# TensorE's program as a loop over images instead of a straight list: a convolution attention and token attention kernel

## The reference, cut to what matters

```python
# layer 0, per image (x: 128 x 1024)
h = group_norm(x, norm_w, norm_b)
q, k, v = split(qkv_w @ h + qkv_b)
x = x + proj_w @ (softmax(q.T k * 128**-0.5) v) + proj_b
# layer 1, on tokens t = x.T (1024 x 128)
sq, sk, rv = heads(ln(t) @ wq_s), heads(ln(t) @ wk_s), heads(ln(t) @ wv_r)   # 8 heads of 16; rv: 2 of 16
retrieved = softmax(sq sk.T / 4) rv                                          # per head, both rv
t = t + mix(softmax over the two of (rq . (retrieved @ wk_ret)), retrieved) @ w_out
t = t + (ln(t) @ w_lora.T) @ ffn_W.T
```

## Time and profile before

| what | value |
|---|---|
| median of 3 runs (lowest, highest) | 4782.99 us (4782.89, 4784.51) |
| the profiled execution, and its span | 4781.04 us, 4779.3 us |
| busy, share of the span: PE, POOL, DVE, ACT | 96%, 89%, 81%, 68% |
| granted TensorE clock, mean | 0.984 of full |

### The profile page before, as it was taken

One profiled execution on the slowest core, in us unless ns is written; L12 is line 12 of the kernel. 1 busy time (PEld: TensorE's weight loads), 2 busy tenths in 40 slices (PEclk: granted clock), 3 DMA queues, 4 the chain that ended last, 5 costly groups with the idle time before them and its releaser, 6 DMA issues.

```text
span 4779.3 us, 95417 instructions
## 1 busy us (share of the span) xinstructions
PE 4587.4 (96%) x29230; PEld 2493.8 (52%) x29230; DVE 3881.3 (81%) x8190; ACT 3242.6 (68%) x6625; POOL 4238.1 (89%) x1142
## 2 busy tenths in 40 slices
PE   5999999999999999999999999999999999999986
PEld 4455555555555555555555555555555555555532
DVE  4788888888888888888888888888888888888773
ACT  2466777766777766777766777766777766777664
POOL 1599999999999999999999999999999999999996
PEclk8899999999999999999999999999999999999987
DMA  1111111111111111111111111111111111111110
GB/s 33 28 41 50 45 32 45 32 45 49 45 32 45 32 45 50 45 32 45 32 45 49 45 32 45 32 45 49 45 32 45 32 45 49 45 32 45 28 41 14
DMA packets 94729, 190.93 MB, mean 40 GB/s; under 512 B 17001, under 2 KB 53481, under 8 KB 94449
## 3 DMA queue, kind: packets, MB, share of 16 engines
q1 hardware_dynamic: 93008, 186.03, 14.0%
q10 hardware_dynamic: 1440, 0.55, 0.0%
HBM read 17.53 MB, written 16.78 MB: 7 GB/s over the span
## 4 chain that ended last, share of the span: by engine, by line
PE 91%; ACT 3%; DVE 2%; POOL 2%; issue 1%; DMA 0%; SPq 0%; ACTq 0%; DVEq 0%; POOLq 0%
PE ps_u L805 19%; PE ps_bank L771 14%; PE ps_bank L791 14%; PE ps_bank L754 10%; PE ps_bank L681 5%; PE ps_bank L692 4%; PE ps_bank L712 3%; PE ps_bank L740 3%; PE ps_bank L814 3%; PE ps_bank L743 3%; PE ps_bank L742 3%; PE ps_bank L741 3%; ACT p L965 2%; POOL p_sum L647 2%; PE ps_bank L723 2%; PE ps_bank L701 2%
## 5 line engine op out<-in xcount | busy, mean ns | idle before, releaser
L647 POOL TENSOR_TENSOR p_sum<-p_sum,p 128x2048 f32<-128x2048 f32 x768 | 3508.4, 4568 | 353.9 <-ACT p L965 306.0
L1085 DVE TENSOR_REDUCE max_part<-ps_bank 128x1 f32<-128x512 f32 x4096 | 2551.3, 681 | 573.5 <-PE ps_bank L771 563.3
L965 ACT ACTIVATE p<-ps_bank 128x512 f32<-128x512 f32 x4096 | 2160.9, 603 | 669.9 <-PE ps_bank L791 653.8
L805 PE MATMUL ps_u<-p,rv 128*32 128x512 f32 x8192 | 996.4, 604 | 0.9 <-ACT p L965 0.9
L771 PE MATMUL ps_bank<-k_stack,q_stack 63*128 63x512 f32 x4096 | 868.9, 452 | 55.2 <-ACT p L965 22.7
L791 PE MATMUL ps_bank<-q_stack,k_stack 64*128 64x512 f32 x4096 | 862.1, 453 | 49.5 <-ACT p L965 29.4
L771 PEld LDWEIGHTS ps_bank<-k_stack,q_stack 63*128 63x128 f32 x4096 | 387.6, 186 | 552.3 <-DVE max_part L1085 244.6
L791 PEld LDWEIGHTS ps_bank<-q_stack,k_stack 64*128 64x128 f32 x4096 | 372.9, 185 | 553.1 <-issue 321.7
L647 POOL TENSOR_TENSOR p_sum<-p 128x2048 f32<-128x2048 f32 x128 | 583.7, 4560 | 66.2 <-ACT p L965 66.2
L754 PE MATMUL ps_bank<-v,p 128*128 128x129 f32 x4096 | 506.8, 277 | 3.1 <-ACT p L920 1.6
L754 PEld LDWEIGHTS ps_bank<-v,p 128*128 128x128 f32 x4096 | 476.0, 191 | 50.1 <-issue 24.0
(11 more groups left out here) (143 smaller groups left out, 4231.8 us busy)
## 6 DMA issues: line engine op xcount, KB each, us to landing
k_stack<-k_hi SPq DMA_DIRECT2D x256, 128.0 KB, 2.6
q_stack<-q_hi SPq DMA_DIRECT2D x256, 128.0 KB, 2.8
x_sb<-in_x SPq DMA_DIRECT2D x32, 512.0 KB, 3.6
k_stack<-k_lo SPq DMA_DIRECT2D x128, 128.0 KB, 2.6
q_stack<-q_lo SPq DMA_DIRECT2D x128, 128.0 KB, 2.9
t_held<-t_front SPq DMA_DIRECT2D x32, 512.0 KB, 3.7
rqk<-tok_next SPq DMA_DIRECT2D x32, 512.0 KB, 3.6
t_core<-t_held SPq DMA_DIRECT2D x32, 512.0 KB, 2.9
```

Of the source, the lines that this page charges most:

```text
L647: pool.tensor_tensor(p_sum[:, phase % 2, :, :], before, p1[:, step % ring, :, :], ALU.add)\
L805: last = pe.matmul(ps_u[n * QUAD:(n + 1) * QUAD, :], rv[:, key_tile, :], p1[:, step % ring, n, :], start=(key_tile == 0), stop=(key_tile = ...
L965: act.activation(p1[:, step % ring, n, :], bank_of("scores", index // 2, n % 2), ACT.Exp, scale=scale1)\
L1085: dve.tensor_reduce(max_part1[:, phase % 2, i, n, half:half + 1], bank_of("max1", index // 2, side), AXIS.X, ALU.max)\
```

## The change

PE's program goes through the same branch of `in_order` as those of the other engines, and the parameter `loop` is gone.

```diff
-def in_order(nc, engine, order, images, stages, banks=None, links=None, section=SECTION, loop=True):
+def in_order(nc, engine, order, images, stages, banks=None, links=None, section=SECTION):
@@
     first = -min(ahead for _, _, ahead, _ in order)
     last = images - 1 - max(ahead for _, _, ahead, _ in order)
-    if not loop:
-        for b in range(last + 1 - images, first + images):
-            turn_of(b)
-        return
     for b in range(last + 1 - images, first):
         turn_of(b)
@@
                     "result": turn("result", t_core, result_ready, halves, out_ready),
-                }, banks, loop=False)
+                }, banks)
```

## The result

| | median (lowest, highest) |
|---|---|
| before | 4783.47 us (4782.16, 4786.09) |
| after | 4805.45 us (4803.32, 4813.21) |
| ratio | 1.0048, 95% interval 1.0038 to 1.0058 |

A forecast was written before the change was run, and what follows sets the result against it. PE was taken to bound the kernel, with 91% of the chain. Held handoffs 25, loop's end 0 and fetching 0 on 4781.0 us gave 4806, as a median 4808; 4807 was given, range 4779 to 4850.

The forecast's parts named there:

- held handoffs: Where PE is held by DVE or ACT: 44 holds a turn at 0.02 us each, 28 turns, 25 us more.
- loop's end: PE's branch behind den: taken as 0, covered by up to 2.8 us of queued array work; 18 us if uncovered.
- What bounds the kernel: Whole kernel: PE bounds it, with 91% of the chain and busy 141.23 of 143.37 us in a middle turn.
- Price of a register instruction: PE's sequencer: at most 0.11 us a step, from below nothing or a gain; 0.02 us taken per hold.
- step c: At held handoffs, the instruction carrying the wait also computes before the matmul: 0 to 0.11 us for each of 44 holds.
- Rival 2, faster: PE's handoffs: at 10 of 44 holds the later wait moves to the load, 31 us saved, 4752; chance 0.07.
- Steps a and b: PE's sequencer: computing ahead of a hold is free; unheld, two register instructions per pair, 0.22 us at most, are just covered.
- Bringing the instructions: PE's instruction queue q8: the 138 KB body is too long to be kept, near 274 packets, costing 0.
- Rival 3, cold branch: PE's branch back: a missing block costs 0.8 us over cover, 22 us more, 4830 (4850 at 4.3 us); chance 0.12.

The follow-up runs named there:

- e4: Kernel before, straight list without loop, each plain wait of PE replaced by a register instruction carrying the same wait: 4763.02 us, ratio 0.9958.
- e7: e4 with a second register instruction behind each one that carries a wait: 4781.01 us, ratio 0.9997.
- e12: Changed kernel with the loop's head at a block's start and the body's waits written in reverse order: 4782.75 us, ratio 0.9997 against before.
- e5: Changed kernel with the loop's first instruction placed at the start of a block of 256: 4766.32 us, ratio 0.9966 against before.
- e2: Changed kernel without the branch hint for PE: 4872.38 us, ratio 1.0184 against before.
- e1: Changed kernel with two turns in PE's loop body, 14 passes instead of 28: 4766.56 us, ratio 0.9964 against before.
- e6: Changed kernel with the loop's first instruction placed 232 into a block of 256: 4777.48 us, ratio 0.9987 against before.
- e3: Changed kernel with the hint moved from the body's head to some 40 instructions ahead of the branch: 4809.72 us, ratio 1.0057 against before.

## Why the prediction was right in number and wrong in reason

| term | forecast | measured |
|---|---|---|
| held handoffs | 28 x 0.88 = +25 | 28 x (142.78 - 143.41) = -17.7 |
| loop's end | 0 | 18 late ends, 1.86 on average = +33.5 |
| clock behind late ends | not seen | 6 x 1.63 = +9.8 |
| sum | +25 | +25.6 (28 turns: +25.4; span: +24.9) |

142.78 is the mean turn of e4; the late ends are each the time from branch to matmul over 2.09 us.

- **What bounds the kernel**: right. PE stays at 141 us of work per turn, and each fraction of a microsecond at a handoff or an edge is felt.
- **Price of a register instruction** (bounds 0 to 0.11, taken 0.02): the size was nearly right, and it was charged to the wrong thing. e7 gives 0.013 a hold for one *more* step. But e12 shows that the exchange of a plain wait for a register instruction costs nothing; a held one even lets the matmul start 0.016 us sooner (0.120 against 0.136).
- **Held handoffs** (step c, "it does more than the plain wait did, since it waits and then computes"): this is the step that failed. I compared what the instruction does, and not which semaphore it holds. The rows of the change, with the sum's semaphore on the sequencer and the bank's on the load at `den` where it had been the other way, showed it.
- **Rival 2, faster**: I had its mechanism word for word ("where the one that ends last moves to the load, the handoff gets shorter by a step"), with 10 places at up to 0.11 us, and 12 at 0.09, less what is given back, were measured. I gave it 0.07 because I took it for a matter of chance which semaphore moves. It isn't: the load carries the wait written last in place of the first (141 of 230 loads name another semaphore), and 12 to 14 of the holds of a turn went to the load with it.
- **Steps a and b** (computing ahead of a hold is free, pairs keep their cover): right. PE's matmuls show no new group of idle between pairs.
- **The loop's end** (0, cover up to 2.8 us): wrong twice. The cover was read from matmul times, from the issue of `den`, but the queue covers 1.7 us. And the price was taken from DVE's loop end, 0.64 us at most, whose body is brought once; PE's isn't.
- **Bringing the instructions** (none kept: 274 packets): that none is kept is right; 311 came, and 284 in e5. The 27 between them are the packets that start around the branch, one at each edge; that they bring the target a second time is inferred from their number and time.
- **Rival 3, cold branch** (4830): mechanism right, place right, seen at 18 ends of 27, 33.5 us and 9.8 with the clock: 43 us. Its own price was 22 us on top of the forecast's 25 (42 at 4.3 us), for branches of the right length but with too long a cover and without the clock. It got 0.12.

Two rivals that exclude one another in the text both came true, and their difference fell on the forecast. Each turn's length would have told them apart at once, and the prediction did ask for that row.

The Trainium skill (Runtime: NRT & Kernel Launch, Instruction fetch mechanics) says that a taken branch whose target isn't among the two blocks held waits for a fetch. Here the trace agrees: 3.3 to 3.9 us at the changed kernel's late ends, up to 5.0 without a hint. It also calls the prefetch purely sequential; e2 and e5 together differ from that, since with the hint, in e5, the target is there at all 27 ends, and without it, in e2, at none.

**What stays open.** That the *place* of the loop in its blocks decides is shown, and the branch's own place fits all runs (some 120, 140, 164 and 178 into a block: no late end in 94 of e1, e6, e5 and e12; some 218: 18 late of 27, and 21 of 27 in e3). Why 218 is bad is argued only: the instructions behind the branch are asked for as well, and push the target out. Where the limit lies wasn't tried, nor why 9 of the 27 ends asked 2 us earlier, nor a body short enough to be kept. Why the clock fell behind 6 of the 18 late ends and not behind the others is open too.

## What to carry to other kernels

When a change swaps the *form* of waits, look at which semaphore ends up on the instruction that starts the work and which on the one ahead of it: the latest one belongs on the work itself, and the order in which waits are written decides it. A loop on the bounding engine whose body isn't kept cost nothing here as long as the target was there when the branch came (e12): give it a hint (67 us between e2 and the changed kernel), and try the place of its head, so that the branch isn't near the end of its block (39 us between the changed kernel and e5) and the head isn't either (11 us between e5 and e6). And read the distribution of turn lengths before believing a mean that agrees with you.

## What the runs showed of the hardware

- From a branch to a block that isn't there, in the changed kernel: about 1.0 us (once 1.5) until the packet starts, 0.9 to 1.4 for the packet, 1.36 until the branch ends, 3.3 to 3.9 in all. With the block there, 0.34 to 0.47; on DVE and ACT, whose loops are kept, 0.05 to 0.06 as a rule.
- An idle of PE of 1.5 to 2.1 us at a late end was followed, 6 times of 18, by a granted clock of 0.50 for some 3.4 us; so was an idle of 1.48 us for a DMA in e5. None of the 9 quick ends was followed by one.
- From a semaphore's rise to the matmul: 0.045 us if the load carries the held wait, 0.120 if a register instruction ahead of it does, 0.136 if a plain wait does. With twelve more holds on the load, e4's turn keeps 0.63 us of some 1.2 won.
